# Metaformer block with a 255-step Runge-Kutta recurrence: the 73 plain steps in three output groups, one group summed by TensorE alone, and half the unused 512-column products

## What is computed

```python
def _mlp(y, W1, b1, W2, b2, W3, b3):
    h = jnp.tanh(y @ W1.T + b1)        # 128 -> 512
    h = jnp.tanh(h @ W2.T + b2)        # 512 -> 512
    return h @ W3.T + b3               # 512 -> 128
k1 = f(y); k2 = f(y + dt/2*k1); k3 = f(y + dt/2*k2); k4 = f(y + dt*k3)
y = y + dt * (k1 + 2*k2 + 2*k3 + k4) / 6
```

## Time and profile before

| what | value |
|---|---|
| median of 3 runs | 2952.32 us (2952.31 to 2953.3) |
| the profiled execution's own time | 2953.22 us |
| its span in the profile | 2951.4 us |
| TensorE busy | 2847.4 us, 96% |
| VectorE busy | 2366.2 us, 80% |
| ScalarE busy | 1417.0 us, 48% |
| mean granted TensorE clock | 0.98 |

### The profile page before, as it was taken

One profiled execution on the slowest core, in us unless ns is written; L12 is line 12 of the kernel. 1 busy time (PEld: TensorE's weight loads), 2 busy tenths in 40 slices (PEclk: granted clock), 3 DMA queues, 4 the chain that ended last, 5 costly groups with the idle time before them and its releaser, 6 DMA issues.

```text
span 2951.4 us, 197650 instructions
## 1 busy us (share of the span) xinstructions
PE 2847.4 (96%) x76994; PEld 2331.3 (79%) x76994; DVE 2366.2 (80%) x12835; ACT 1417.0 (48%) x8958; POOL 587.9 (20%) x903
## 2 busy tenths in 40 slices
PE   7789999999999999999999999999999999999999
PEld 3478888888888888888888878888887777777777
DVE  4668888888888888888888878888877777777777
ACT  5455555555555555565554444444433333333333
POOL 5023232332323323233331001111100000000000
PEclk9779999999999999999999999999999999999999
DMA  3000000000000000000000000000000000000000
GB/s 115 0 12 11 11 14 11 14 11 11 14 11 14 11 12 13 11 14 11 14 11 5 0 0 1 0 0 0 8 8 0 0 0 0 0 0 0 0 0 14
DMA packets 21977, 28.15 MB, mean 10 GB/s; under 512 B 4384, under 2 KB 12896, under 8 KB 21544
## 3 DMA queue, kind: packets, MB, share of 16 engines
q1 hardware_dynamic: 21928, 27.48, 3.0%
HBM read 25.24 MB, written 2.23 MB: 9 GB/s over the span
## 4 chain that ended last, share of the span: by engine, by line
PE 88%; DVE 5%; ACT 4%; issue 2%; DMA 0%; SPq 0%; DVEq 0%; ACTq 0%; POOLq 0%; POOL 0%
PE PSUM L616 32%; PE PSUM L622 28%; PE PSUM L677 12%; PE PSUM L607 6%; PE PSUM L684 4%; DVE PSUM L1234 3%; ACT HA L934 2%; PE PSUM L714 1%; PE PSUM L643 1%; PE PSUM L647 1%; PE PSUM L454 1%; PE PSUM L448 0%; PE PSUM L656 0%; PE PSUM L486 0%; PE PSUM L690 0%
## 5 line engine op out<-in xcount | busy, mean ns | idle before, releaser
L1234 DVE TENSOR_REDUCE PSUM<-PSUM 128x32 f32<-128x64 f32 x4080 | 872.4, 232 | 168.5 <-PE PSUM L622 114.7
L616 PEld LDWEIGHTS PSUM<-HA,RL 128*128 128x128 f16 x16320 | 553.5, 96 | 306.2 <-ACT HA L934 297.0
L935 ACT ACTIVATE PSUM<-PSUM 128x32 f32<-128x32 f32 x4080 | 786.4, 194 | 0.0
L934 ACT ACTIVATE HA<-PSUM 128x32 f16<-128x32 f32 x2040 | 404.9, 199 | 722.6 <-DVE PSUM L1234 722.5
L934 ACT ACTIVATE HB<-PSUM 128x32 f16<-128x32 f32 x2040 | 405.1, 200 | 714.6 <-DVE PSUM L1234 714.6
L616 PE MATMUL PSUM<-HA,RL 128*128 128x16 f16 x16320 | 718.1, 170 | 31.2 <-ACT HA L934 7.5
L616 PE MATMUL PSUM<-HB,RLU 128*128 128x16 f16 x16320 | 716.8, 170 | 6.8 <-ACT HB L934 0.2
L622 PE MATMUL PSUM<-HA,RH 128*128 128x32 f16 x16320 | 652.9, 177 | 0.0
L622 PE MATMUL PSUM<-HB,RHU 128*128 128x32 f16 x16320 | 651.8, 177 | 0.0
L616 PEld LDWEIGHTS PSUM<-HB,RLU 128*128 128x128 f16 x16320 | 550.8, 96 | 71.9 <-ACT HB L934 2.4
L622 PEld LDWEIGHTS PSUM<-HA,RH 128*128 128x128 f16 x16320 | 566.0, 96 | 0.0
(11 more groups left out here) (229 smaller groups left out, 3071.5 us busy)
## 6 DMA issues: line engine op xcount, KB each, us to landing
G<-scores SPq DMA_DIRECT2D x64, 256.0 KB, 3.1
N<-in_x SPq DMA_DIRECT2D x8, 256.0 KB, 4.6
NHL<-in_w SPq DMA_DIRECT2D x1, 2048.0 KB, 10.4
STF<-in_w SPq DMA_DIRECT2D x1, 2048.0 KB, 15.1
out<-W2HL SPq DMA_DIRECT2D x8, 256.0 KB, 2.4
G<-in_r SPq DMA_DIRECT2D x1, 1024.0 KB, 5.4
R1K<-in_r SPq DMA_DIRECT2D x1, 256.0 KB, 2.7
R3F<-in_r SPq DMA_DIRECT2D x1, 256.0 KB, 5.6
```

The source lines that it names most:

```text
L616: mm(out[m // 2][:, 2 * B * (m % 2):2 * B * (m % 2) + B], lo[:, k, m], src[:, k, 0], start=False, stop=False)
L934: A(hi[:, 2 * h:2 * h + 2, 0], src, ACT.Tanh, scale=1.0 / scale).then_inc(rk_hi, 1)
L935: A(full, src, ACT.Tanh, scale=1.0 / scale).then_inc(rk_f, 1)
L1234: v.tensor_reduce(bank[:, SUM:SUM + 2 * B].rearrange("p (m b) -> p m b", m=2), bank[:, 0:4 * B].rearrange("p (m c b) -> p m b c", m=2, c=2 ...
```

## The change

In the 73 plain steps:

- The outputs stand in three groups, m 0 / m 1 and 2 / m 3, each in a bank of its own (banks 0 to 2 for one layer's sums, 5 to 7 for the other's), with semaphores of their own (`sp_p`, `sp_r`, `sp_hi`, `sp_f`, `sp_lo`).
- Block 0 is written to 16 columns only: all its products (kinds L, h and l, 16 columns each) accumulate in the same place, so no reduction is needed and ScalarE waits for TensorE itself. It takes 12 products in place of 8, and a layer 36 in place of 32.
- The order of the 36 products is a list (`SPLIT_ORDER`). In it L is low weights by high input, h and l are high weights by the high or the low input (16 columns), H is both (32 columns); then k and m.
- Injections are four products per injected term (16, 16, 64 and 32 columns) in place of two.
- The unused 512-column product stays ahead of layer 0 and goes ahead of layer 1.
- VectorE and ScalarE work on three groups: two reductions, three subtractions, six tanh per layer, in place of two, two and four.
- VectorE's subtraction for HSS (L1215) moves from the next layer 0 to behind the copy of layer 1 at j = 0.
- VectorE's loop covers eight steps per pass (nine passes, after one step ahead of them that opens with the old form); TensorE, ScalarE and GpSimd keep a loop of one step per pass.

```diff
+SPREAD, OFFSET = 336, 176
+SPLIT = ((0,), (1, 2), (3,))
+SPLIT_OF = (0, 1, 1, 2)
+SPLIT_ORDER = [(w[0], int(w[1]), int(w[2])) for w in (
+    "L03 L01 h00 L02 L00 h10 h20 L12 L20 H01 L11 l00 L21 L31 H02 L22 L30 H11 H12 L10 H21 H22 l20 L32 H31 H32 l30 h30 "
+    "l10 L33 L23 H13 L13 H23 H33 H03").split()]
...
             with pe.Fori(0, OG) as i:
                 step(S_OUT + i, False, lambda slot, i=i: give(i, slot))
-            with pe.Fori(S_PLAIN, STEPS) as s:
-                step(s, False, lambda slot: keep_clock())
+            def split_inject(lay, ident, what, start):
+                for half in range(2):
+                    mm(SPLIT_SUM[lay][:, 0], ident[:, :], what[:, 0, half], start=start and half == 0, stop=False)
+                mm(PAIRED[lay][0], ident[:, :], what[:, 1:3], start=start, stop=False)
+                mm(PAIRED[lay][1], ident[:, :], what[:, 3], start=start, stop=False)
...
+            def split_layer(s, j, lay, hi, lo, src, opening):
+                waited = set()
+                for i, (kind, k, m) in enumerate(SPLIT_ORDER):
+                    low_half, group = kind in "lH", k // 2 if opening else SPLIT_OF[k]
+                    if (low_half, group) not in waited:
+                        waited.add((low_half, group))
...
+                            pe.wait_ge((sp_lo if low_half else sp_hi)[group], split_count(s, j, lay))
+                    ends = all(SPLIT_OF[m] != SPLIT_OF[b] for _, _, b in SPLIT_ORDER[i + 1:])
...
+                    if ends:
+                        t.then_inc(sp_p[SPLIT_OF[m]], 1)
+
+            def split_step(s, opening):
+                for j in range(4):
+                    pe.wait_ge(rk_s, 4 * s + j)
+                    split_inject(1, IDV, CI[:, 3], True)
+                    warm()
+                    split_layer(s, j, 0, RH2, RL2, HA, opening and j == 0)
...
+                    if j < 3:
+                        pe.wait_ge(rk_u, 4 * s + j + 1)
+                        split_inject(0, IDU, CI[:, COEF_OF[j]], True)
+                        split_inject(0, IDU, UI, False)
...
+                    split_layer(s, j, 1, RHU[:, COEF_OF[j]], RLU[:, COEF_OF[j]], HB, False)
+
+            split_step(S_PLAIN, True)
+            with pe.Fori(S_PLAIN + 1, STEPS) as s:
+                split_step(s, False)
...
+                        for g, ms in enumerate(SPLIT):
+                            act.wait_ge((sp_r if g else sp_p)[g], split_count(s, j, lay))
+                            sl = slice(ms[0], ms[-1] + 1)
+                            A(hi[:, sl, 0], SPLIT_SUM[lay][:, sl], ACT.Tanh, scale=1.0 / scale).then_inc(sp_hi[g], 1)
+                            A(SPLIT_FULL[lay][:, sl], SPLIT_SUM[lay][:, sl], ACT.Tanh, scale=1.0 / scale).then_inc(sp_f[g], 1)
...
+                            for g in (1, 2):
+                                ms = SPLIT[g]
+                                dve.wait_ge(sp_p[g], split_count(s, j, lay))
+                                v.tensor_reduce(SPLIT_SUM[lay][:, ms[0]:ms[-1] + 1],
+                                                PAIRED[lay][g - 1].rearrange("p (m c b) -> p m b c", m=len(ms), c=2),
+                                                AX.X, ALU.add).then_inc(sp_r[g], 1)
+                            for g, ms in enumerate(SPLIT):
+                                dve.wait_ge(sp_f[g], split_count(s, j, lay))
+                                sl = slice(ms[0], ms[-1] + 1)
+                                TT(hi[:, sl, 1], full[:, sl], hi[:, sl, 0], ALU.subtract).then_inc(sp_lo[g], 1)
...
+            split_step(S_PLAIN, True)
+            with dve.Fori(0, (STEPS - S_PLAIN - 1) // 8) as n:
+                for r in range(8):
+                    split_step(S_PLAIN + 1 + 8 * n + r, False)
```

More of the change, by code:

```diff
@@ L244, in build, with split_count, spread @@
         rk_s, rk_hs, rk_k, rk_yd, rk_y, rk_ys = (sem("rk_" + k) for k in ("s", "hs", "k", "yd", "y", "ys"))
+        sp_p, sp_r, sp_hi, sp_f, sp_lo = ([sem(f"sp_{k}{g}") for g in range(3)] for k in ("p", "r", "hi", "f", "lo"))
+        def split_count(s, j, lay):
+            return 8 * (s - S_PLAIN) + 2 * j + lay
+        def spread(lay, column):
+            flat = PSUM[:, 5 * lay:5 * lay + 3].rearrange("p k n -> p (k n)")[:, column:column + MC * SPREAD]
+            return flat.rearrange("p (m x) -> p m x", m=MC)[:, :, 0:B]
+        SPLIT_SUM, SPLIT_FULL = (tuple(spread(lay, OFFSET + c) for lay in range(2)) for c in (0, B))
+        PAIRED = tuple((PS[5 * lay + 1][:, 2 * B:6 * B], PS[5 * lay + 2][:, 0:2 * B]) for lay in range(2))
         o_s, o_tr, o_c, o_out = (sem("o_" + k) for k in ("s", "tr", "c", "out"))
@@ L961, in _, with split_step @@
                 step(S_OUT + i, False, lambda slot, i=i: give(i, slot))
-            with act.Fori(S_PLAIN, STEPS) as s:
-                step(s, False)
+            def split_step(s, opening):
+                for j in range(4):
+                    for lay, hi, scale in ((0, HA, SCALE_U), (1, HB, SCALE_V)):
+                        if opening and j == 0 and lay == 0:
+                            for h in range(2):
+                                act.wait_ge(rk_r, count(s, j, lay, h))
+                                src, full = (PSUM[:, h, c:c + 2 * B].rearrange("p (m b) -> p m b", m=2) for c in (SUM, FULL))
+                                A(hi[:, 2 * h:2 * h + 2, 0], src, ACT.Tanh, scale=1.0 / scale).then_inc(rk_hi, 1)
+                                A(full, src, ACT.Tanh, scale=1.0 / scale).then_inc(rk_f, 1)
+                            continue
+                        for g, ms in enumerate(SPLIT):
[4 more added lines that the diff above has]
+            split_step(S_PLAIN, True)
+            with act.Fori(S_PLAIN + 1, STEPS) as s:
+                split_step(s, False)
             for i in range(OG):
```

84 lines of the change are left out of this document (83 added, 1 removed).

## The result

The changed kernel takes **2996.18 us** (median of 4 runs, 2992.67 to 2997.29) where the kernel before takes 2952.81: a ratio of 1.0143, interval 1.013 to 1.0155. It is 43 us slower; forecast were 2906 us, 2901 to 2940. The profiled execution took 2996.77 us.

A forecast was written before the change was run, and what follows sets the result against it. The recurrence's loop of 1.335 us per layer, not an engine's capacity, was taken as the bound. Gains of 43.8 (layers) and 5.1 (loop), less 1.6 (jumps) and 0.8, made 46.5: 2952.3 to 2906 us, range 2901 to 2940.

The forecast's parts named there:

- The layer: Each layer of the plain steps was to fall from 1.335 to 1.26 us, set by the second group's loop.
- The third group's price: Loop through output block m 3: 1.25 us taken, its half-wide operations saving 0.08; without any saving 1.335, today's layer.
- 584 x 0.075: Gain over the stage's 584 layers at 0.075 us each: 43.8 us.
- Loop on VectorE: Eight steps per pass remove 64 of 72 branches at step ends, 0.08 us each: 5.1 us gained.
- TensorE's own time: TensorE's products, injections and unused product take 1.22 us before layer 0 and at most 1.21 before layer 1, below 1.26.
- I take 0.2: Extra cost of each far jump of VectorE's loop, between bounds of 0 and 1.7 us; eight jumps cost 1.6 us.
- rival B: VectorE's far jump re-reads its code, 1.7 us at each of eight jumps: 2918 us; chance 0.17.
- needed there: Removing the unused product ahead of layer 1 avoids a layer of 1.33 us; not a gain by itself.
- Rival C: With fewer unused products the clock falls to 0.50: 46 us slower, 2998 us; chance 0.09 for over half the stage.
- short whiles: Milder case of the falling clock, low for short whiles only: 2910 to 2945 us; chance 0.13.
- over half: Clock at 0.50 for over half of the stage, the case of 2998 us; chance 0.09.
- The two rules: Skill rules weighed: code beyond 512 instructions stalls at a jump, giving 2918; matmuls without long idle gaps hold the clock.

The follow-up runs named there:

- loop8_w512: The changed kernel with a 512-column unused product ahead of layer 1 as well, VectorE's loop still eight steps; 2972.39 us, ratio 1.0065.
- loop2_fit: The changed kernel with VectorE's loop over two steps and unused products of 256, 128, 128, 256 columns ahead of layer 1; 2917.01 us, ratio 0.9874.
- before_loop8: The kernel before with only VectorE's loop changed, to eight steps per pass; 2978.64 us, ratio 1.0085.
- loop4: The changed kernel with VectorE's loop over four steps per pass in place of eight; 3028.25 us, ratio 1.0253.
- loop4_w256: loop4 with an unused product of 256 columns ahead of layer 1 as well; 2989.46 us, ratio 1.0119.
- before_half: The kernel before with its unused 512-column product in the plain steps only ahead of layer 0, every second layer; 2970.55 us, ratio 1.0053.
- loop1: The changed kernel with VectorE's loop over one step per pass; 2934.26 us, ratio 0.9938.
- loop2: The changed kernel with VectorE's loop over two steps per pass; 2932.69 us, ratio 0.9941.
- written_out: The changed kernel with VectorE's 72 plain steps written out one behind another, no loop; 2932.03 us, ratio 0.9919.
- loop2_none: The changed kernel with VectorE's loop over two steps and no unused product in the plain steps; 2940.47 us, ratio 0.9954.
- fit_edge256: loop2_fit with the unused product at each step's start cut from 512 to 256 columns; 2910.5 us, ratio 0.9861.

## Why the prediction was wrong

Three terms failed, and together they are the 90 us between 2906 and 2996: the clock, taken as 1.00 with one 512-column product in every two layers (some 60 us), the far jumps at 0.2 each (19 us more than forecast), and the branch of TensorE's loop, which had no term (12 us). The sum of the layer held.

- **The layer: right.** "1.26 us" for the second group and all below it for the rest: the first tanh of each layer stand 1.26 apart at full clock, released by TensorE. The third group's price did not decide: TensorE waits a little for the second group's parts and not for the third's low part. In layer 0 TensorE's own stream, 1.22 by the forecast, is within 0.04 of the layer, so there was nearly no room below 1.26 in any case. That a product left ahead of layer 1 gives 1.33 was right too (loop8_w512: 1.327). The gain of 584 x 0.075 is there in loop2_fit: 2917 us, which with the next two points is the forecast.
- **"Loop on VectorE", the gain: right for the old schedule, of no use in the new.** before_loop8 shows 1.34 where 1.42 stood. But with a layer of 1.26 TensorE has no spare time at a step's end: its own branch (0.2 us on its queue) delays the injections, the 512 columns pass that on, and the first layer is 1.43. The forecast counted "TensorE's own time" for 1.22 in a layer and forgot that its loop too has an end: 73 x 0.17 = 12.4 us. That is a term left out. 2906 + 12.4 - 1.6, the price of far jumps that it has not, is 2916.8, against 2917.0 for loop2_fit, whose kernel before took 1.5 us more than the forecast's.
- **"I take 0.2", the far jump: wrong.** It is 2.6 to 2.7 a jump, 21 us in place of 1.6. The argument was that q14's 16 reads show that loops are hardly read again; true of loops of one step, and said nothing of one eight times as long. The bound of 1.7, the landing of a small transfer, was too low as well; what a jump does beyond one such read isn't shown. The Trainium skill, "Runtime: NRT & Kernel Launch", "Instruction fetch mechanics", had the mechanism right, and rival B deserved more than 0.17; but its 512 instructions are not the length that a loop may have here: loop4's pass, some 280 instructions of VectorE (half of the 562 rows of eight steps), is under them and stalled at each of its 17 jumps, with 104 reads. A pass of two steps, some 140, did not. The same section says that they are refilled in blocks of 256; whether a pass longer than one block is what stalls, no run here shows.
- **The clock, 1.00 throughout: wrong, the largest part.** The forecast called the removal of the 512-column product ahead of layer 1 "needed there" and left the clock out of its sum. Rival C, 0.09, is what happened. Its prices were right to 0.02 (1.52 and 1.31 to 1.33; a step of 11.54 against the 11.4 forecast, by the step's edge), its extent not: "short whiles" had more chance than "over half". The low clock makes the step 11.54 against 10.27, and 0.66 of 73 steps x 1.27 is 61 us. That the missing product is behind it is shown by loop8_w512 (0.98 where the changed kernel has 0.67), loop4_w256 against loop4 (0.91, 0.62) and before_half against before (0.78, 1.00). With 2917 and 21 for the stalls that gives 2999 for the measured 2996.
- **Why so long.** The forecast took B and C for independent, each alone. They are not: with the product in every second layer and no far jumps the clock is low for 0.10 of the stretch in the profiled executions of loop1 and loop2, their fastest, and for 0.36 in that of written_out, its slowest; with jumps for 0.66, and for 0.76 with twice as many (loop4). Both rivals in one run was a case that it did not have.
- **The two rules.** On the clock the trace of before was right against the rule, and more was to be had from it than was taken: the earlier trace rows showed TensorE busy 12.95 of 13.70 us at 0.50. loop2_none, busy 729 of 730 and at 0.50 throughout, is the same at full length. The Trainium skill, "TensorE: Matmul & The Clock Gate", "Why this matters for your kernels", asks for no idle gaps; by the profile's busy time loop2_none shows that this is not enough.

Undoing each part, from the changed kernel and by ratios: no jumps -60 us (loop2), of which 21 are the stalls themselves and the rest the clock; products that fit ahead of layer 1 a further -20, clock at 1.00 throughout; TensorE's loop of two -5.

## What to carry to other kernels

A product that looks unused can hold the clock: when one is removed, read the granted clock where the old trace runs the same work without it, and give the new schedule's spare time back as unused products, sized layer by layer to fit. Unroll a loop by two or write it out whole: of the sizes tried here, the ones between (four and eight steps, 280 and 560 instructions) jump to code that has to be read again. And when a loop's body gets shorter, list every engine's branch anew: what was hidden before may now be on the path.

## What the runs showed of the hardware

- A jump back over about 280 or 560 VectorE instructions stalls it for 2.7 to 3.1 us; back over some 140 it does not (q14 18); straight code of some 4100 runs without a layer above 2 us, while q14 reads it (48 reads in the run, 128 instructions each).
- TensorE at 0.50 prices by width: the 512 columns hold up what follows for 0.38 instead of 0.21, but the small products of a layer start 0.027 apart instead of 0.025 (layers without the long product 1.31 to 1.33 against 1.26).
- Near the edge the clock is not repeatable: loop1, loop2 and written_out spread over 11 to 19 us in four runs; loop2_fit, at 1.00 throughout, over 1.4. In loop1 the order of the times is that of the mean clocks (2927.65 us at 0.965, 2931.94 at 0.956, 2936.57 at 0.953, 2938.84 at 0.946). A spread alone is a weaker sign: fit_edge256 spreads over 7 us, by one run, with clocks of 0.977 to 0.979.
